# Attention inside a two-layer kernel: normalisation and value copy on ScalarE, the value bias folded into the output bias

## The reference, cut to what matters

```python
def proj(x, w, b):
    y = x @ w.T + b
    return y.reshape(B, S, H, D_K).transpose(0, 2, 1, 3)      # H = 16 heads of D_K = 16
Q = proj(q, wq_w, wq_b)
K = proj(k, wk_w, wk_b)
V = proj(v, wv_w, wv_b)
scores = einsum('bhqd,bhkd->bhqk', Q, K) / sqrt(D_K)
scores = where(mask == 0, 1e-09, scores)
attn = softmax(scores, axis=-1)
out = einsum('bhqk,bhkd->bhqd', attn, V)
out = out.transpose(0, 2, 1, 3).reshape(B, S, H * D_K)
return out @ wo_w.T + wo_b
...
x = x + xattn(_layernorm(x), ctx, ctx, mask, ...)
```

## Time and profile before

| | us |
|---|---|
| median of 3 runs | 1572.52 (1570.85 to 1574.6) |
| the profiled execution | 1573.39 |
| its span, first to last instruction | 1571.7 |
| attention stage within the span | about 816 to 1215 |
| the first mask and the last reciprocal of the stage | 847.1 and 1211.3 |

### The profile page before, as it was taken

How to read it: one execution, slowest core, us unless ns; L and a number is a source line. 1 busy time by engine, 2 the same in 40 slices (tenths; PEclk the granted TensorE clock), 3 DMA queues, 4 the chain that set the end, 5 groups by cost and what they waited for, 6 DMA issues and landing times. The chain is left out here.

```text
span 1571.7 us, 31820 instructions
## 1 busy us (share of the span) xinstructions
PE 1283.2 (82%) x10494; PEld 1043.0 (66%) x10495; DVE 1159.7 (74%) x2040; ACT 840.5 (53%) x1282; POOL 472.0 (30%) x491
## 2 busy tenths in 40 slices
PE   6989999999999772999935999999997498750087
PEld 3458888888888631888834888888887254220076
DVE  2869865555656466996527999999996696998844
ACT  4856533333333231663304667676763667877664
POOL 3234755545554303355321223223223000000000
PEclk9999999999999985999975889998986699995599
DMA  9887633323232275673234010000000101337211
GB/s 320 309 260 216 155 52 53 46 49 51 44 54 38 30 235 164 184 215 52 35 65 145 21 28 20 27 27 20 27 15 1 40 1 41 144 124 259 75 52 57
DMA packets 108871, 147.32 MB, mean 94 GB/s; under 512 B 17136, under 2 KB 84720, under 8 KB 106992
## 3 DMA queue, kind: packets, MB, share of 16 engines
q1 hardware_dynamic: 87280, 116.31, 22.5%
q0 software_dynamic: 21504, 29.83, 11.4%
HBM read 92.62 MB, written 53.49 MB: 93 GB/s over the span
## 5 line engine op out<-in xcount | busy, mean ns | idle before, releaser
L734 ACT ACTIVATE top_x_all<-top_h_ps,top_b1T 128x256 f32<-128x256 f32 x448 | 184.5, 474 | 303.9 <-PE top_h_ps L580 296.1
L580 PE MATMUL top_h_ps<-top_xT_hi,top_w_lo 128*128 128x256 f16 x896 | 245.3, 274 | 1.2 <-issue 1.2
L578 PE MATMUL top_h_ps<-top_xT_hi,top_w_hi 128*128 128x256 f16 x896 | 245.4, 274 | 0.9 <-issue 0.9
L579 PE MATMUL top_h_ps<-top_xT_lo,top_w_hi 128*128 128x256 f16 x896 | 245.4, 274 | 0.0
L596 PE MATMUL top_y_ps<-top_w_hi,top_x_all 128*128 x896 | 244.2, 273 | 0.2 <-DVE top_x_all L933 0.2
L598 PE MATMUL top_y_ps<-top_w_hi,top_x_all 128*128 x896 | 244.2, 273 | 0.0
L597 PE MATMUL top_y_ps<-top_w_lo,top_x_all 128*128 x896 | 244.2, 273 | 0.0
L931 DVE CAST top_x_all<-top_x_all 128x512 f16<-128x512 f32 x224 | 98.1, 438 | 150.0 <-ACT top_x_all L734 146.3
L933 DVE TENSOR_TENSOR top_x_all<-top_x_all 128x512 f16<-128x512 f32 x224 | 155.8, 695 | 7.7
L387 POOL DMA_INDIRECT x_sum<-top_x_all,top_row_of_slot x56 | 96.2, 1718 | 178.7 <-DVE top_x_all L945 155.9
L1742 PE MATMUL ffn_ps<-ffn_dT_hi,ffn_yT 128*128 128x256 f16 x192 | 53.8, 280 | 91.1 <-DVE ffn_yT L2022 91.1
(11 more groups left out here) (321 smaller groups left out, 3118.3 us busy)
## 6 DMA issues: line engine op xcount, KB each, us to landing
top_staged<-in_L_xattn_W SPq DMA_DIRECT2D x32, 512.0 KB
top_staged<-in_L_ffn_w SPq DMA_DIRECT2D x32, 512.0 KB
up_raw<-ffn_u_all SPq DMA_DIRECT2D x48, 256.0 KB, 2.1
ffn_yT<-up_raw SPq DMA_DIRECT2D x12, 1024.0 KB, 4.7
kv_rows<-top_w_lo SPq DMA_DIRECT2D x32, 256.0 KB, 4.3
attn_kv_in<-kv_rows SPq DMA_DIRECT2D x32, 256.0 KB, 2.6
top_w_lo<-in_ctx SPq DMA_DIRECT2D x4, 1024.0 KB, 10.3
top_x_all<-in_x SPq DMA_DIRECT2D x4, 1024.0 KB, 12.0
```

The source lines that it names most:

```text
L578: nc.tensor.matmul(out, hi, xT_hi[p][:, c, :], start=(c == 0), stop=False)
L579: nc.tensor.matmul(out, hi, xT_lo[p][:, c, :], start=False, stop=False)
L580: last = nc.tensor.matmul(out, lo, xT_hi[p][:, c, :], start=False, stop=(c == DC - 1))
L734: last = nc.scalar.activation(h32[:, fc * R:(fc + 1) * R], h_ps[:, b, q * R:(q + 1) * R], ACT.Relu, bias=b1T[:, bass.ds(e * FC + fc, 1)], ...
```

## The change

Four things change in the attention stage, and nothing elsewhere.

1. The normalisation moves from VectorE (`(x - mean) * rstd`) to ScalarE (`rstd * x + shift`), to the end of ScalarE's slot. VectorE makes `shift = -mean * rstd` once for the first 8 tiles and once for the other 24.
2. The values are copied into their tile on ScalarE, ahead of the normalisation, without their bias. On VectorE `value_bias` is gone.
3. At the start the value bias is transposed (TensorE), split (VectorE), multiplied by the output weights (TensorE, six products), and added to the output bias (VectorE).
4. GpSimd waits for this new output bias before its first tile, and TensorE waits for it before the first key transposes, since these overwrite the PSUM tile in which the product stands.

```diff
@@ constants and semaphores
+        shift = sb("shift", [P, B], F32)
+        bvT = [sb(f"bvT_{k}", [P, DC, P], F16) for k in ("hi", "lo")]
...
@@ GpSimd
-            pool.wait_ge(s_w, 16 * 7)
+            pool.wait_ge(s_bo, 1)
@@ TensorE, at the start, and output_bias in between(-2)
             pe.wait_ge(s_prep, 1)
+            for c in range(DC):
+                mm = nc.tensor.transpose(front[1][:, D + c * P:D + (c + 1) * P], biases[:, 2, c * P:(c + 1) * P], ident[:])
+            mm.then_inc(s_bvt, 1)
+
+            def output_bias(n):
+                if n == -2:
+                    pe.wait_ge(s_bv, 1)
+                    for c in range(DC):
+                        nc.tensor.matmul(front[1][:, 0:D], bvT[0][:, c, :], wT_hi[:, 1, c, :], start=(c == 0), stop=False)
+                        nc.tensor.matmul(front[1][:, 0:D], bvT[0][:, c, :], wT_lo[:, 1, c, :], start=False, stop=False)
+                        mm = nc.tensor.matmul(front[1][:, 0:D], bvT[1][:, c, :], wT_hi[:, 1, c, :], start=False, stop=(c == DC - 1))
+                    mm.then_inc(s_bvp, 1)
...
             def key_transposes(m, p, i):
                 this(pe, s_kl, m, p)
 
+                if isinstance(m, int) and m == 0 and p == 0:
+                    pe.wait_ge(s_bo, 1)
@@ ScalarE
+            def normalise(m, p, i):
+                b = 2 * m + p
+                if isinstance(m, int):
+                    act.wait_ge(s_scales, 1 if b < QB else 2)
+
+                last(act, s_tp, m, p)
+                A.activation(xn[:], x_all[:, bass.ds(b, 1), :].rearrange("p a d -> p (a d)"), ACT.Identity,
+                             bias=shift[:, bass.ds(b, 1)], scale=rstd[:, bass.ds(b, 1)]).then_inc(s_xn[p], 1)
+
+            def value_copy(m, p, i):
+                act.wait_ge(s_c[p], 16 * (m + 1))
...
+                A.activation(v32[i][:, :, 0:DK], kv_in[p][:, D:2 * D].rearrange("p (h d) -> p h d", h=H), ACT.Copy).then_inc(s_v32[p], 1)
...
                 on(exps, 0, 1)
+                on(value_copy, 2)
+                on(normalise, 3)
@@ VectorE
+            def value_bias_split():
+                dve.wait_ge(s_bvt, 1)
+                rows = front[1][:, D:2 * D].rearrange("p (c t) -> p c t", c=DC)
+                order(V.tensor_copy(bvT[0][:], rows))
+                V.tensor_tensor(bvT[1][:], rows, bvT[0][:], ALU.subtract).then_inc(s_bv, 1)
...
                 order(V.tensor_tensor(r, r, w, ALU.mult))
+                V.scalar_tensor_tensor(shift[:, tiles], mean_var[:, tiles, 0], -1.0, r, ALU.mult, ALU.mult).then_inc(s_scales, 1)
...
             def between(n):
+                if n == -3:
+                    value_bias_split()
+                if n == -2:
+                    output_bias()
...
-                V.tensor_scalar(xn[:], x_all[:, bass.ds(b, 1), :].rearrange("p a d -> p (a d)"),
-                                mean_var[:, bass.ds(b, 1), 0], rstd[:, bass.ds(b, 1)], ALU.subtract, ALU.mult).then_inc(s_xn[p], 1)
+            def output_bias():
+                dve.wait_ge(s_bvp, 1)
+                V.scalar_tensor_tensor(biases[:, 3, :], front[1][:, 0:D], 1 / WEIGHT_SCALE, biases[:, 3, :],
+                                       ALU.mult, ALU.add).then_inc(s_bo, 1)
...
-            def value_bias(m, p, i):
-                dve.wait_ge(s_c[p], 16 * (m + 1))
-                V.tensor_tensor(v32[i][:, :, 0:DK], kv_in[p][:, D:2 * D].rearrange("p (h d) -> p h d", h=H),
-                                biases[:, 2, :].rearrange("p (h d) -> p h d", h=H), ALU.add).then_inc(s_v32[p], 1)
...
-                on(value_bias, 2)
                 on(softmax_mask, 0, 1)
...
-                on(normalise, 3)
                 on(divide, -1)
```

More of the change, by code:

```diff
@@ L1060, in attention @@
         s_pool = sem("pool_order"); s_dve = sem("dve_order"); s_const = sem("constants")
-        s_var = sem("variance"); s_root = sem("root"); s_prep = sem("dve_prepared")
+        s_var = sem("variance"); s_root = sem("root"); s_scales = sem("norm_scales"); s_bvt = sem("value_bias_transposed"); s_bv = sem("value_bias_split"); s_bvp = sem("value_bias_product"); s_bo = sem("output_bias_ready"); s_prep = sem("dve_prepared")
         s_wt = two("weights_transposed"); s_wh = two("weights_hi"); s_wl = two("weights_lo")
@@ L1284, in slot @@
                 on(value_products, -1, 1)
-            slots(pe, slot)
+            slots(pe, slot, output_bias)
         @block.scalar
@@ L1308, in front_in @@
                 A.activation(inT_hi[:].rearrange("p c t -> p (c t)"), front[0][:, 0:D], ACT.Copy).then_inc(s_th[p], 1)
+            def normalise(m, p, i):
[7 more added lines that the diff above has]
+                act.wait_ge(s_c[p], 16 * (m + 1))
+                if isinstance(m, int):
+                    act.wait_ge(s_const, 7)
+                A.activation(v32[i][:, :, 0:DK], kv_in[p][:, D:2 * D].rearrange("p (h d) -> p h d", h=H), ACT.Copy).then_inc(s_v32[p], 1)
             def query_high(m, p, i):
@@ L1407, in between @@
                     V.reciprocal(g_inv[:], g_scale[:]).then_inc(s_gscale, 1)
-            def normalise(m, p, i):
-                b = 2 * m + p
-                last(dve, s_tp, m, p)
-                V.tensor_scalar(xn[:], x_all[:, bass.ds(b, 1), :].rearrange("p a d -> p (a d)"),
-                                mean_var[:, bass.ds(b, 1), 0], rstd[:, bass.ds(b, 1)], ALU.subtract, ALU.mult).then_inc(s_xn[p], 1)
+            def output_bias():
+                dve.wait_ge(s_bvp, 1)
+                V.scalar_tensor_tensor(biases[:, 3, :], front[1][:, 0:D], 1 / WEIGHT_SCALE, biases[:, 3, :],
+                                       ALU.mult, ALU.add).then_inc(s_bo, 1)
             def front_low(m, p, i):
```

## The result

The changed kernel took 1560.3 us in the median of 6 runs (1558.49 to 1563.77); the kernel before, run beside it, 1572.21 (1568.84 to 1574.6). The ratio is 0.9922, with a 95% interval from 0.9908 to 0.9936: 12 us faster, where 2 had been forecast. The profiled execution took 1558.49 us, the fastest of the six, and 14.9 less than the profiled one of before.

What follows compares the result with a forecast made beforehand. The prediction took a loop through VectorE, ScalarE and TensorE as the bound. Its terms, +0.17 - 0.33 + 0.20 - 2.1 = -2.1 us, took the median 1572.52 to 1570.4 us; the range for 8 in 10 was 1563 to 1576.

Steps and rivals of the forecast that it cites:

- The loop: Attention stage, reciprocal through exponential, row transpose and value product to next reciprocal: 0.11 us gained in 18 tiles, 2.1 us.
- D: Attention stage: ScalarE doesn't hide the added work; 0.3 us in 25 slots, 7.5 us slower, 1577.9; chance 0.03.
- 1.88 of cover: ScalarE's idle time per slot, waiting for TensorE's transposes: 1.88 us, claimed to hide the added 0.99 us at no cost.
- The start: Start of the attention stage: added preparation makes the first query product 0.5 us late, the first mask 0.17 us later.
- Rival A: Attention stage: VectorE alone sets the pace; 18 slots give 0.65 us each, 11.7 us, so 1560.8 us; chance 0.12.
- the forecast's own count of long slots: Inner slots of the attention stage: 11 of 25 over 11.1 us, assumed to change by one or two low stretches.
- rival B: Attention stage: fewer stretches at TensorE's low clock; half gone gives 1565.4 us, all gone 12 us; chance 0.19.

Runs made afterwards that it cites:

- e1: The kernel before with only the normalisation moved to ScalarE, the value bias staying on VectorE: 1561.64 us, ratio 0.9925 to the kernel before.
- e2: The kernel before with only the value copy moved to ScalarE, its bias folded into the output bias: 1562.79 us, ratio 0.9935.
- e5: The kernel before with three idle products on TensorE ahead of the query transposes in each slot: 1562.08 us, ratio 0.9939.
- e12: The kernel before with row statistics ahead of the reciprocal and three idle products at each of two places in TensorE's slot: 1564.84 us.
- e10: The changed kernel with row statistics ahead of the reciprocal and three idle products at each of two places in TensorE's slot: 1555.91 us.
- e4: The changed kernel with VectorE's row statistics ahead of the reciprocal instead of behind the division: 1560.24 us, ratio 0.9923 to the kernel before.
- e8: The changed kernel with four tiny memsets on VectorE behind the row statistics, inside the loop: 1570.67 us, ratio 0.9996 to the kernel before.
- e9: The changed kernel with e8's four memsets and three idle products on TensorE ahead of the query transposes: 1564.4 us, ratio 0.9933.
- e7: The changed kernel with row statistics ahead of the reciprocal and three idle products on TensorE at one place, ahead of the query transposes: 1558.08 us.

## Why the prediction was wrong

The mechanism was right, term by term; one term, which the forecast held at zero, was most of the result.

- *The loop.* Predicted: slots 10.2 us apart, about 0.5 us of wait at the reciprocal in nearly all tiles, that wait above 20 us in sum. Measured: 10.21, 0.45 in most tiles, 20.8 us in 32. Its gain of 0.11 us a slot was predicted for 18 tiles (2.1 us); it came in every clean slot, since the slots that had been long became clean ones (2.75 in 25). VectorE's busy time was to fall by more than 20 us and fell by 19.0.
- *ScalarE.* Predicted 0.59 and 0.40 us, with 0.38 to 0.62 for the copy; measured 0.61 and 0.43. The wait ahead of the first probability copy went to 1.14 us (about 1.1 predicted). D is out. Its price was also worked out wrong: 0.99 us doubled is 0.10 over the 1.88 of cover, 2.5 us in 25 slots, and not 0.3 and 7.5.
- *The start.* Six products in 1.28 us (1.25 predicted), the shift 0.17 (0.2). The first query product starts 7.53 us after the first statistics, where it was 7.07: 0.46 later, against 0.5. The first mask was to come 0.17 later and came 0.24 earlier, 17.33 against 17.57 us behind the first statistics.
- *Rival A* has the measured time, 1560.8, and is wrong all the same. Its sign, slots of 9.7 us with no wait at the reciprocal, isn't there, and e1, e2 and e5 show that VectorE's load isn't what the time follows. A number alone would have crowned it. The Trainium skill ("Perfetto Trace Analysis", "Identifying the Most-Contended Engine") led to it; e12 against e10 shows it at its best here, with 0.39 of 0.65 us.
- **The step that failed** is the forecast's own count of long slots: "one or two low stretches more or fewer" of 11. Nine went in the inner stretch, worth 6.9 us of the two profiled executions, and the last slots may have given up to 2.9 more, a stretch that the sum didn't price at all. That is rival B at its far end ("with all gone, 12 us"), and its sign, a count clearly under 11, is there. B had 0.19, and the range left out its far end. The prediction had named the cause, that a slot 0.11 us shorter moves where the stretches fall, and then treated the count as nearly fixed. Nothing in the rows bore that out: 11 of the inner slots were long and 14 not, in a pattern that comes back every seven or eight slots. So strict a pattern suggests that the length of the slot sets it, and then a shift of that length can move all of it. The range should have reached both ends, from 1560 to beyond 1577.
- The Trainium skill ("TensorE: Matmul & The Clock Gate", "What's actually happening") says that activity releases the throttle. TensorE's busy share can't test that here: it was 94% before (253.06 of 269.69 us) at a clock of 0.93 and 92% after (239.72 of 260.18) at 0.98, but the same products take longer at the low clock, so the share rises where the clock falls. Two runs can. e5 agrees: more activity in TensorE's wait took 8 of 11 long slots away. e4 doesn't: it does the same products in slots of 9.93 us instead of 10.21, and has 7 long slots instead of 2.

What is shown: that low stretches, not VectorE's load, carry most of the gain (e1, e2, e5), and that four memsets worth 0.05 us a slot bring them back, which idle products on TensorE undo (e8, e9). What stays open: whether it is the slot's length that does it, why 10.21 us is then clean and 9.93, 10.26 and 10.32 are not, and whether the change has a part in the shorter end of the stage. The experiments give no rule that would have told it ahead.

## What to carry to other kernels

When a loop's iterations fall into two lengths and TensorE's granted clock differs between them, an edit's worth is its effect on the loop plus a term for the low stretches that can be larger and of either sign; give that term the full width of its count. Before judging edits of a tenth of a microsecond, try to take the clock out of the comparison, by filling TensorE's waits with products that nobody reads, and read the granted clock to see whether it worked: here one place was enough for e5 and not for e7, and no filling settled the end of the stage. Work taken from the busiest engine is worth only the distance to the next chain behind it: 0.11 of 0.65 us a slot here, and 0.39 once that chain had been made shorter.

## What the runs showed of the hardware

- 0.05 us on a slot of 10.21 us (e8) took the inner slots over 11 us from 2 to 9 in the profiled executions, and the median from 1560.3 to 1570.67.
- The end of the stage, from the 28th to the last reciprocal, took 42.8 to 43.7 us or 46.4 to 48.7 in 14 profiles, at a clock of 0.83 to 0.90 or 0.68 to 0.74.
- Three idle products a slot, of 0.48 us together, made an otherwise unchanged kernel 0.61% faster (e5): 1562.08 against 1572.86 us.
- Four memsets of 2 columns share a row of 0.09 us in the timeline (0.06 us each, overlapping), and lengthened the slot by 0.05 us in all (e8).
